# Expert tiles of a mixture-of-experts layer: four of hid's six chunks transposed by VectorE in 32x32 blocks, their low parts made by GpSimd

## The chip, the cores and the metric

The program runs on one core of a Trainium2 chip. The metric is the device time in microseconds from launch to end, the median of three runs. A profiled execution of the same program stands beside it; its span is the time from the first to the last instruction.

## The reference

A Flamingo-style block on 4 x 1024 tokens of width 256: layer norm, gated cross attention to 77 context rows, layer norm, and a feed-forward part in which each token goes to 2 of 4 experts of inner width 688, beside a shared expert. The part at issue is the routed experts:

```python
scores = softmax(xf @ gate_w.T)
topk_w, topk_idx = top_k(scores, 2)            # weights scaled to sum 1
g = silu(einsum('nh,eih->eni', xf, eg))
u = einsum('nh,eih->eni', xf, eu)
y_exp = einsum('eni,ehi->enh', g * u, ed)
y = einsum('enh,ne->nh', y_exp, comb) + shared expert
out = x + tanh(g_ffn) * y
```

## The kernel before

The first part of the program (up to about 480 us) does the attention, the shared expert and the routing table, and transposes the experts' weights into SBUF. Then `routed` works through NS = 67 tiles of 128 token slots, each with one expert. All matrix products are fp32 taken apart into a high part (rounded to fp32r) and a low part (what is left), three passes per product: high x high, high x low weights, low x high.

One tile j goes through these steps, and every engine has its own program with the steps of all tiles in order:

- GpSimd (`on_gpsimd`): `gather(j)` copies the tile's slot numbers and issues an indirect DMA that brings 128 rows into `xin[k]` (two buffers); it waits for the transposes of tile j-2 (`s_xT`).
- TensorE: `x_T(j)` transposes `xin` into PSUM (2 transposes). ScalarE: `x_hi` copies the high part; VectorE: `x_lo` subtracts the low part.
- TensorE: `gate_up(j)`, 18 matmuls into three PSUM banks. ScalarE: `sil`. VectorE: `hid` = up x sil, 128 x 688, and a second copy of the last 48 columns (`s_dup`).
- TensorE: `hidden_T(j)`, six transposes of `hid`'s chunks of 128 columns into `p_h` (four in bank 0, two in bank 1). ScalarE copies the high parts, L252 (four chunks) and L253 (two); VectorE subtracts the low parts, L298 (four chunks), L300 and L302, and then raises `s_hlo`.
- TensorE: `down(j)`, 17 matmuls of 256 columns into `p_y`. VectorE: `result(j)` (L277) scales by the slot weights into `yout[k]`. GpSimd: `add(j)` copies the slot numbers and issues an indirect DMA that adds `yout` to the output rows in HBM.

The order on TensorE in step j is `gate_up(j)`, `x_T(j+1)`, `down(j-1)`, `hidden_T(j)`. On VectorE it is `hid(j)`, `x_lo(j+1)`, `result(j-1)`, the low parts of tile j. On ScalarE it is `sil(j)`, `x_hi(j+1)`, the high parts of tile j. On GpSimd the order is `add(j)`, `gather(j+4)`, `add(j+1)`, `gather(j+5)`. Nothing reorders these; the code is written out by hand with semaphores, and tiles 2 to 65 run in a loop on each engine whose body has two tiles.

The names of the trace differ at places from those of the code, since tensors share memory: `p_gu` is shown as `p_s`, `p_x` as `p_m`, `p_h` as `p_f`, `p_y` as `p_t`.

Of the kernel before, what the change touches and what calls it, by code (L numbers as in the profile page):

```python
# [8 lines left out]
ALU = mybir.AluOpType  # L9
ACT = mybir.ActivationFunctionType  # L10
AX = mybir.AxisListType

P = 128

B, S, H = 4, 1024, 256
# [34 lines left out]
NE = N * TOPK // P  # L50
EG = 8
# [85 lines left out]
def routed(nc, v, sem, place, banks):  # L137
# [12 lines left out]
    hT = [sb(f"hT_{s}", [P, n, P], f32r) for s, n in (("hi", FC), ("lo", FC - 1))]  # L150
    p_gu, p_x, p_h, p_y = banks
    names = ("s_xT s_xhi s_xlo s_gu s_sil s_hid s_hT s_hhi s_hlo s_y s_yo s_pad "
             "s_get_at s_add_at s_add").split()
    (s_xT, s_xhi, s_xlo, s_gu, s_sil, s_hid, s_hT, s_hhi, s_hlo, s_y, s_yo, s_pad,
     s_get_at, s_add_at, s_add) = (sem("f" + n) for n in names)
# [37 lines left out]
    def on_gpsimd(pool, s_rows_out):  # L193
        gather = gathers(pool)

        def add(j, k):
            wait(pool, s_add, 16 * (j - 1))
            pool.tensor_copy(add_at[k][:, :], slot_id[:, bass.ds(j, 1)]).then_inc(s_add_at, 1)
            pool.wait_ge(s_add_at, j + 1)
            pool.wait_ge(s_yo, j + 1)  # L200

            wait(pool, s_add, 16 * j)
            settle(pool)
            pool.indirect_dma_start(out, bass.IndirectOffsetOnAxis(add_at[k][:, :], 0),  # L204
                                    yout[k][:, :], None, compute_op=ALU.add).then_inc(s_add, 16)

        gather(2, 0)
        for j in range(2):
            gather(j + 3, 1 - j)
            if j == 0:  # L210
                for s in s_rows_out:
                    pool.wait_ge(s, 16 * (NU // 2))
            add(j, j)
        with pool.Fori(1, (NS - 3) // 2) as h:
            for k in range(2):
                gather(2 * h + k + 3, 1 - k)
                add(2 * h + k, k)
        for j in range((NS - 3) // 2 * 2, NS):
            if j + 3 < NS:
                gather(j + 3, 1 - j % 2)  # L220
            add(j, j % 2)
        pool.wait_ge(s_add, 16 * NS)
# [11 lines left out]
    def on_scalar(act, down_high):  # L234
        x_hi = x_high(act)

        def step(j, k):
# [10 lines left out]
            if first:  # L248
# [3 lines left out]
            act.activation(hT[0][:, 0:4, :], p_h[0][:, :].rearrange("p (c t) -> p c t", t=P), ACT.Copy)  # L252
            act.activation(hT[0][:, 4:FC, :], p_h[1][:, 0:2 * P].rearrange("p (c t) -> p c t", t=P),  # L253
                           ACT.Copy).then_inc(s_hhi, 1)
            if first:
                down_high(2)
# [14 lines left out]
    def on_vector(dve, down_low):  # L271
# [7 lines left out]

        def step(j, k):  # L280
            last = isinstance(j, int) and j == NS - 1
            dve.wait_ge(s_sil, j + 1)
            wait(dve, s_hT, j)
            nc.vector.tensor_tensor(hid[:, 0:FF], p_gu[:, FF:2 * FF], sil[:, :], ALU.mult).then_inc(s_hid, 1)  # L284
# [10 lines left out]
            else:  # L295
                result(j - 1, 1 - k)
            dve.wait_ge(s_hhi, j + 1)
            nc.vector.tensor_tensor(hT[1][:, 0:4, :], p_h[0][:, :].rearrange("p (c t) -> p c t", t=P),  # L298
                                    hT[0][:, 0:4, :], ALU.subtract)
# [3 lines left out]
                                    hT[0][LO_AT:P, FC - 1, :], ALU.subtract).then_inc(s_hlo, 1)  # L303
            if first:
                down_low(2)
# [13 lines left out]
    def on_tensor(pe, down_weights, down_ready):  # L319
# [14 lines left out]
        def down(j, e):  # L334
            pe.wait_ge(s_hlo, j + 1)
            wait(pe, s_yo, j)
            for c in range(FC - 1):
                for q, (a, b) in enumerate(PASSES):
                    nc.tensor.matmul(p_y[:, 0:H], hT[a][:, c, :], wd[b][:, bass.ds(e * FC + c, 1), :],  # L339
                                     start=(c == 0 and q == 0), stop=False)  # L340

            for b in range(2):
                last = nc.tensor.matmul(p_y[:, 0:H], hT[0][:, FC - 1, :],  # L343
                                        wd[b][:, bass.ds(e * FC + FC - 1, 1), :], start=False, stop=(b == 1))
            last.then_inc(s_y, 1)

        def hidden_T(j):
            pe.wait_ge(s_hid, j + 1)
            wait(pe, s_hlo, j)
            for c in range(FC):  # L350
# [2064 lines left out]
```

## Time and profile before

| | us |
|---|---|
| median of 3 runs | 945.41 (942.92 to 946.67) |
| the profiled execution, its own time | 943.28 |
| its span | 941.3 |
| mean granted TensorE clock, share of full | 0.98 |
| busy in the span: TensorE / VectorE / ScalarE / GpSimd | 890.7 / 574.7 / 476.0 / 467.9 |
| busy in the 100 us from 700 to 800: TensorE / VectorE / ScalarE / GpSimd | 100.00 / 45.47 / 28.74 / 45.52 |

"PE" in the rows is TensorE's matmuls (a transpose is a matmul too), DVE is VectorE, ACT ScalarE, POOL GpSimd. A row of the timeline gives the start, the duration, the engine, the line of the kernel, the operation, the output and the input, and in brackets how long the engine had been idle before it and what ended that. Matmuls are pipelined, so their durations overlap: the chain of waits gives the time by which each one moves the chain on, which is the better measure of what they cost.

### The profile page before, as it was taken

Reading aid. Unit: us, or ns where it says so; the run is one execution under the profiler, and the core shown is the slowest. Engines: PE = TensorE matmul, PEld = TensorE weight load, DVE = VectorE, ACT = ScalarE, POOL = GpSimd, SP = SyncE. Lnnn points to the kernel's source line nnn. Section 1 sums busy time; section 2 is a strip of 40 time slices with the busy share of each in tenths; the row PEclk is TensorE's granted clock in tenths of the full one; section 3 lists DMA queues with packets and bytes.
Section 4 is the critical chain, followed back from the end, with each engine's and each line's share of the span. In section 5 each row is a group of like instructions: output and inputs, shape, how many; then the busy total and the mean of one; then the engine's idle time right before and its main releaser. Section 6 shows DMA issues by size and latency. Waiting matters only on the chain.

```text
span 941.3 us, 21873 instructions
## 1 busy us (share of the span) xinstructions
PE 890.7 (95%) x6491; PEld 797.3 (85%) x6492; DVE 574.7 (61%) x1289; ACT 476.0 (51%) x1804; POOL 467.9 (50%) x643
## 2 busy tenths in 40 slices
PE   6789999999999899998889999999999999999995
PEld 4567788888888798998779999999999999999994
DVE  5788889889888477776634444444444444444442
ACT  3999899899898234565523222222223222222221
POOL 4566667577556233667313444444444444444442
PEclk9899999999999899999989999999999999999997
DMA  5135122223212213142222222222222222222221
GB/s 178 28 120 159 61 84 88 89 74 104 64 55 92 90 36 127 65 128 87 96 71 34 39 39 39 39 45 33 45 35 43 39 39 39 39 45 33 45 37 20
DMA packets 56863, 61.72 MB, mean 66 GB/s; under 512 B 15642, under 2 KB 45183, under 8 KB 56799
## 3 DMA queue, kind: packets, MB, share of 16 engines
q1 hardware_dynamic: 42871, 43.15, 14.5%
q0 software_dynamic: 12864, 17.57, 11.3%
q8 instruction: 32, 0.52, 0.2%
q10 hardware_dynamic: 1064, 0.21, 0.1%
q14 instruction: 32, 0.26, 0.1%
HBM read 34.78 MB, written 25.82 MB: 64 GB/s over the span
## 4 chain that ended last, share of the span: by engine, by line
PE 77%; DVE 8%; ACT 6%; issue 5%; POOL 2%; DMA 1%; DVEq 0%; ACTq 0%; SPq 0%; POOLq 0%
PE p_s L329 27%; PE p_t L339 13%; PE p_f L2038 5%; PE p_f L353 5%; PE p_f L2083 4%; ACT prob L1106 3%; PE p_m L1995 3%; PE p_s L1968 2%; PE p_m L2007 2%; PE p_t L1980 2%; PE p_s L2038 2%; PE p_t L343 2%; PE p_m L1949 2%; PE p_m L314 2%; DVE xn L1450 1%
## 5 line engine op out<-in xcount | busy, mean ns | idle before, releaser
L204 POOL DMA_INDIRECT out_rows<-yout,add_at x67 | 107.1, 1598 | 196.1 <-DVE yout L277 196.1
L1106 ACT ACTIVATE prob<-p_s,negmax 128x77 f32<-128x77 f32 x512 | 161.7, 385 | 0.3
L284 DVE TENSOR_TENSOR hid<-p_s,sil 128x688 f32<-128x688 f32 x67 | 58.6, 875 | 165.7 <-ACT sil L242 105.6
L242 ACT ACTIVATE sil<-p_s 128x688 f32<-128x688 f32 x67 | 49.9, 745 | 196.1 <-PE p_s L329 196.1
L1106 ACT ACTIVATION_READ_ACCUMULATOR prob<-p_s,negmax 128x1 f32 x512 | 131.9, 269 | 0.0
L837 POOL TENSOR_TENSOR prob<-prob,rinv 128x616 f32<-128x616 f32 x64 | 78.4, 1228 | 82.9 <-DVE rinv L1494 82.9
L329 PE MATMUL p_s<-wgu_hi,fxT_hi 128*128 x402 | 111.4, 385 | 1.8 <-DVE hid L269 1.8
L329 PE MATMUL p_s<-wgu_lo,fxT_hi 128*128 x402 | 105.7, 371 | 0.0
L329 PE MATMUL p_s<-wgu_hi,fxT_lo 128*128 x402 | 105.1, 370 | 0.0
L252 ACT ACTIVATE hT_hi<-p_f 128x512 fp32r<-128x512 f32 x67 | 40.0, 597 | 124.1 <-PE p_f L353 124.1
L339 PE MATMUL p_t<-wd_hi,hT_hi 128*128 x335 | 99.5, 297 | 2.3 <-DVE hT_hi L302 2.3
L188 POOL DMA_INDIRECT xin<-xn_scratch,get_at x67 | 67.7, 1010 | 55.5 <-POOL get_at L185 51.6
L339 PE MATMUL p_t<-wd_hi,hT_lo 128*128 x335 | 94.7, 283 | 0.0
L339 PE MATMUL p_t<-wd_lo,hT_hi 128*128 x335 | 94.5, 282 | 0.0
L329 PEld LDWEIGHTS p_s<-wgu_hi,fxT_lo 128*128 128x128 f32 x402 | 72.4, 189 | 11.5
L329 PEld LDWEIGHTS p_s<-wgu_lo,fxT_hi 128*128 128x128 f32 x402 | 72.4, 189 | 11.2
L298 DVE TENSOR_TENSOR hT_lo<-p_f,hT_hi 128x512 fp32r<-128x512 f32 x67 | 46.4, 692 | 58.1 <-ACT hT_hi L253 58.1
L856 POOL TENSOR_TENSOR shT_lo<-shid,shT_hi 128x256 fp32r<-128x256 f32 x80 | 59.0, 747 | 43.9 <-ACT shT_hi L1146 43.9
L2038 PE MATMUL p_f<-xnT_hi,swgu_hi 128*128 128x256 f32 x248 | 78.2, 315 | 0.8 <-DVE shid L1509 0.8
L329 PEld LDWEIGHTS p_s<-wgu_hi,fxT_hi 128*128 128x128 f32 x402 | 69.1, 190 | 10.7 <-issue 2.0
L2038 PE MATMUL p_f<-xnT_hi,swgu_lo 128*128 128x256 f32 x248 | 70.2, 283 | 0.0
L2038 PE MATMUL p_f<-xnT_lo,swgu_hi 128*128 128x256 f32 x248 | 70.1, 283 | 0.0
(253 smaller groups left out, 2453.0 us busy)
## 6 DMA issues: line engine op xcount, KB each, us to landing
xr<-in_x SPq DMA_DIRECT2D x16, 256.0 KB, 3.1
x_scratch<-xr SPq DMA_DIRECT2D x16, 256.0 KB, 2.4
xn_scratch<-xn SPq DMA_DIRECT2D x16, 256.0 KB, 2.1
xt_scratch<-xnT SPq DMA_DIRECT2D x16, 256.0 KB, 2.1
xin<-xt_scratch SPq DMA_DIRECT2D x16, 256.0 KB, 3.3
x1in<-x_scratch SPq DMA_DIRECT2D x16, 256.0 KB, 3.1
out_rows<-syout SPq DMA_DIRECT2D x16, 256.0 KB, 2.5
raw<-in_L_ffn_ed SPq DMA_DIRECT2D x4, 688.0 KB, 4.2
```

Source lines behind the costliest of these rows:

```text
L188: pool.indirect_dma_start(xin[k][:, :], None, xn_d, bass.IndirectOffsetOnAxis(get_at[k][:, :], 0)).then_inc(s_gat[k], 16)
L204: pool.indirect_dma_start(out, bass.IndirectOffsetOnAxis(add_at[k][:, :], 0), yout[k][:, :], None, compute_op=ALU.add).then_inc(s_add, 16)
L242: act.activation(sil[:, :], p_gu[:, 0:FF], ACT.Silu).then_inc(s_sil, 1)
L284: nc.vector.tensor_tensor(hid[:, 0:FF], p_gu[:, FF:2 * FF], sil[:, :], ALU.mult).then_inc(s_hid, 1)
L298: nc.vector.tensor_tensor(hT[1][:, 0:4, :], p_h[0][:, :].rearrange("p (c t) -> p c t", t=P), hT[0][:, 0:4, :], ALU.subtract)
L329: last = nc.tensor.matmul(p_gu[:, g0:g1], fxT[a][:, c, :], wgu[b][:, bass.ds(e * KC + c, 1), g0:g1], start=(c == 0 and q == 0), stop=(c == ...
L339: nc.tensor.matmul(p_y[:, 0:H], hT[a][:, c, :], wd[b][:, bass.ds(e * FC + c, 1), :], start=(c == 0 and q == 0), stop=False)
L353: last = nc.tensor.transpose(p_h[c // 4][:, (c % 4) * P:(c % 4 + 1) * P], hid[:, c * P:(c + 1) * P], ident[:, :])
L837: pool.tensor_tensor(pr_, pr_, rinv[:, t, m * HH:(m + 1) * HH].unsqueeze(2).broadcast_to([P, HH, SK]), ALU.mult).then_inc(s_P, 1)
L856: pool.tensor_tensor(hT[1][:, c, :], hid[:, c, :], hT[0][:, c, :], ALU.subtract).then_inc(s_hlo, 1)
L1106: last = act.activation(prob[n % 2][t][:, m * PW + h * SK:m * PW + (h + 1) * SK], p_s[:, 2 * t + h // 4, col:col + SK], ACT.Exp, bias=negm ...
L2038: last = nc.tensor.matmul(bank[:, j * UT * P:(j + 1) * UT * P], swgu[w][:, k, j * SGU + c * P:j * SGU + (c + 1) * P], xns[x][:, n % 2, k, ...
```

## The change

Four of the six chunks (BY_DVE = 4) are no longer transposed by TensorE, apart from those of the last tile. VectorE does it in `squares(j)`, right behind `result(j-1)`: sixteen instructions, each of which takes 32 partitions and, in all four chunks, 32 columns, and writes them transposed into `hT32`, an SBUF tile of 128 x 512. ScalarE copies the high part from `hT32` (behind the two other chunks, and after `s_square`). GpSimd subtracts the low part in `wide_lo(j)`, which stands between `gather(j+2)` and `add(j-1)`. TensorE's `down(j)` starts with the two chunks that TensorE transposed, goes on with the high parts of the four after `s_hhi`, and ends with their four low parts after `s_wide_lo`; the number of matmuls is 17 as before. VectorE's two small subtractions, which raise `s_hlo`, stand behind the sixteen transposes. In the first tile and in the last, pieces of this order differ as the diff shows.

```diff
@@ -48,6 +48,8 @@
 
 XR = 6
 NE = N * TOPK // P
+BY_DVE = 4
+SQ = 32
 EG = 8
 NSP = NS + 1
 
@@ -204,9 +207,16 @@
             pool.indirect_dma_start(out, bass.IndirectOffsetOnAxis(add_at[k][:, :], 0),
                                     yout[k][:, :], None, compute_op=ALU.add).then_inc(s_add, 16)
 
+        def wide_lo(j):
+            pool.wait_ge(s_hhi, 2 * j + 2)
+            pool.tensor_tensor(hT[1][:, 0:BY_DVE, :], hT32[:, :, :], hT[0][:, 0:BY_DVE, :],
+                               ALU.subtract).then_inc(s_wide_lo, 1)
+
         gather(2, 0)
+        wide_lo(0)
         for j in range(2):
             gather(j + 3, 1 - j)
+            wide_lo(j + 1)
             if j == 0:
                 for s in s_rows_out:
                     pool.wait_ge(s, 16 * (NU // 2))
@@ -214,10 +224,13 @@
         with pool.Fori(1, (NS - 3) // 2) as h:
             for k in range(2):
                 gather(2 * h + k + 3, 1 - k)
+                wide_lo(2 * h + k + 1)
                 add(2 * h + k, k)
         for j in range((NS - 3) // 2 * 2, NS):
             if j + 3 < NS:
                 gather(j + 3, 1 - j % 2)
+            if j + 1 < NS - 1:
+                wide_lo(j + 1)
             add(j, j % 2)
         pool.wait_ge(s_add, 16 * NS)
 
@@ -249,9 +262,14 @@
                 down_high(1)
 
             act.wait_ge(s_hT, j + 1)
-            act.activation(hT[0][:, 0:4, :], p_h[0][:, :].rearrange("p (c t) -> p c t", t=P), ACT.Copy)
-            act.activation(hT[0][:, 4:FC, :], p_h[1][:, 0:2 * P].rearrange("p (c t) -> p c t", t=P),
+            act.activation(hT[0][:, BY_DVE:FC, :], p_h[1][:, 0:2 * P].rearrange("p (c t) -> p c t", t=P),
                            ACT.Copy).then_inc(s_hhi, 1)
+            if last:
+                act.activation(hT[0][:, 0:BY_DVE, :], p_h[0][:, :].rearrange("p (c t) -> p c t", t=P),
+                               ACT.Copy).then_inc(s_hhi, 1)
+            else:
+                act.wait_ge(s_square, j + 1)
+                act.activation(hT[0][:, 0:BY_DVE, :], hT32[:, :, :], ACT.Copy).then_inc(s_hhi, 1)
             if first:
                 down_high(2)
 
@@ -277,10 +295,20 @@
             nc.vector.tensor_scalar(yout[k][:, :], p_y[:, 0:H], slots[:, bass.ds(j, 1)], None,
                                     ALU.mult).then_inc(s_yo, 1)
 
+        def squares(j):
+            dve.wait_ge(s_hid, j + 1)
+            wait(dve, s_wide_lo, j)
+            src = hid[:, 0:BY_DVE * P].rearrange("p (c i) -> p c i", i=P)
+            for a in range(0, P, SQ):
+                for b in range(0, P, SQ):
+                    done = nc.vector.transpose(out=hT32[b:b + SQ, :, a:a + SQ], in_=src[a:a + SQ, :, b:b + SQ])
+            done.then_inc(s_square, 1)
+
         def step(j, k):
             last = isinstance(j, int) and j == NS - 1
             dve.wait_ge(s_sil, j + 1)
             wait(dve, s_hT, j)
+            wait(dve, s_square, j)
             nc.vector.tensor_tensor(hid[:, 0:FF], p_gu[:, FF:2 * FF], sil[:, :], ALU.mult).then_inc(s_hid, 1)
 
             nc.vector.tensor_tensor(hid[:, (FC - 1) * P + LO_AT:(FC - 1) * P + LO_AT + FT],
@@ -294,13 +322,17 @@
                 down_low(1)
             else:
                 result(j - 1, 1 - k)
-            dve.wait_ge(s_hhi, j + 1)
-            nc.vector.tensor_tensor(hT[1][:, 0:4, :], p_h[0][:, :].rearrange("p (c t) -> p c t", t=P),
-                                    hT[0][:, 0:4, :], ALU.subtract)
+            if not last:
+                squares(j)
+            dve.wait_ge(s_hhi, 2 * j + 1)
             nc.vector.tensor_tensor(hT[1][:, 4, :], p_h[1][:, 0:P], hT[0][:, 4, :], ALU.subtract)
 
             nc.vector.tensor_tensor(hT[0][LO_AT:P, FC - 1, :], p_h[1][LO_AT:P, P:2 * P],
                                     hT[0][LO_AT:P, FC - 1, :], ALU.subtract).then_inc(s_hlo, 1)
+            if last:
+                dve.wait_ge(s_hhi, 2 * j + 2)
+                nc.vector.tensor_tensor(hT[1][:, 0:BY_DVE, :], p_h[0][:, :].rearrange("p (c t) -> p c t", t=P),
+                                        hT[0][:, 0:BY_DVE, :], ALU.subtract).then_inc(s_wide_lo, 1)
             if first:
                 down_low(2)
         tiles(dve, step)
@@ -334,20 +366,27 @@
         def down(j, e):
             pe.wait_ge(s_hlo, j + 1)
             wait(pe, s_yo, j)
-            for c in range(FC - 1):
-                for q, (a, b) in enumerate(PASSES):
-                    nc.tensor.matmul(p_y[:, 0:H], hT[a][:, c, :], wd[b][:, bass.ds(e * FC + c, 1), :],
-                                     start=(c == 0 and q == 0), stop=False)
-
+            for q, (a, b) in enumerate(PASSES):
+                nc.tensor.matmul(p_y[:, 0:H], hT[a][:, FC - 2, :], wd[b][:, bass.ds(e * FC + FC - 2, 1), :],
+                                 start=(q == 0), stop=False)
             for b in range(2):
-                last = nc.tensor.matmul(p_y[:, 0:H], hT[0][:, FC - 1, :],
-                                        wd[b][:, bass.ds(e * FC + FC - 1, 1), :], start=False, stop=(b == 1))
+                nc.tensor.matmul(p_y[:, 0:H], hT[0][:, FC - 1, :], wd[b][:, bass.ds(e * FC + FC - 1, 1), :],
+                                 start=False, stop=False)
+            pe.wait_ge(s_hhi, 2 * j + 2)
+            for c in range(BY_DVE):
+                for b in range(2):
+                    nc.tensor.matmul(p_y[:, 0:H], hT[0][:, c, :], wd[b][:, bass.ds(e * FC + c, 1), :],
+                                     start=False, stop=False)
+            pe.wait_ge(s_wide_lo, j + 1)
+            for c in range(BY_DVE):
+                last = nc.tensor.matmul(p_y[:, 0:H], hT[1][:, c, :], wd[0][:, bass.ds(e * FC + c, 1), :],
+                                        start=False, stop=(c == BY_DVE - 1))
             last.then_inc(s_y, 1)
 
         def hidden_T(j):
             pe.wait_ge(s_hid, j + 1)
             wait(pe, s_hlo, j)
-            for c in range(FC):
+            for c in range(0 if isinstance(j, int) and j == NS - 1 else BY_DVE, FC):
                 if c == FC - 1:
                     pe.wait_ge(s_dup, j + 1)
                 last = nc.tensor.transpose(p_h[c // 4][:, (c % 4) * P:(c % 4 + 1) * P], hid[:, c * P:(c + 1) * P],
```

The program of VectorE around one tile of the loop, before (names as in the trace; `yout_177` and `yout_178` are the two `yout` buffers):

```order
L284 TENSOR_TENSOR hid<-p_s,sil 128x688 [waits fs_hT,fs_sil]
L286 TENSOR_TENSOR hid<-p_s,sil 128x48
L262 REGISTER_ALU
L263 TENSOR_TENSOR fxT_lo<-p_m,fxT_hi 128x256 [waits fs_xhi]
L174 ISA [waits fs_y]
L277 ISA [waits fs_add]
L277 TENSOR_SCALAR yout_178<-p_t,slots 128x256
L298 TENSOR_TENSOR hT_lo<-p_f,hT_hi 128x512 [waits fs_hhi]
L300 TENSOR_TENSOR hT_lo<-p_f,hT_hi 128x128
L302 TENSOR_TENSOR hT_hi<-p_f,hT_hi 64x128
```

And the same place with the change (`hT_189` is `hT32`):

```order
L312 TENSOR_TENSOR hid<-p_s,sil 128x688 [waits fs_square,fs_hT,fs_sil]
L314 TENSOR_TENSOR hid<-p_s,sil 128x48
L280 REGISTER_ALU
L281 TENSOR_TENSOR fxT_lo<-p_m,fxT_hi 128x256 [waits fs_xhi]
L177 REGISTER_ALU [waits fs_y]
L295 ISA [waits fs_add]
L295 TENSOR_SCALAR yout_177<-p_t,slots 128x256
L304 STREAM_TRANSPOSE hT_189<-hid 32x4x32 [waits fs_wide_lo,fs_hid]
L304 STREAM_TRANSPOSE hT_189<-hid 32x4x32 x15
L327 ISA
L328 TENSOR_TENSOR hT_lo<-p_f,hT_hi 128x128 [waits fs_hhi]
L330 TENSOR_TENSOR hT_hi<-p_f,hT_hi 64x128
L167 REGISTER_ALU
```

The large subtraction of 512 columns is gone and the sixteen transposes stand in its place, ahead of the two small subtractions that they had stood behind.

GpSimd's program for one tile of the loop, before (`xin`, `get_at`: the gather; `yout`, `add_at`: the add):

```order
L185 ISA [waits fs_xT]
L185 COPY get_at_182<-slot_id 128x1
L186 REGISTER_ALU
L188 DMA xin_175<-xn_scratch,get_at_182 128x256 [waits fs_get_at]
L198 ISA [waits fs_add]
L198 COPY add_at_185<-slot_id 128x1
L174 REGISTER_ALU [waits fs_yo,fs_add_at]
L204 DMA out_rows<-yout_178,add_at_185 4224x256 [waits fs_add]
```

And with the change:

```order
L188 ISA [waits fs_xT]
L188 COPY get_at_182<-slot_id 128x1
L189 REGISTER_ALU
L191 DMA xin_175<-xn_scratch,get_at_182 128x256 [waits fs_get_at]
L211 ISA
L212 TENSOR_TENSOR hT_lo<-hT_189,hT_hi 128x512 [waits fs_hhi]
L201 ISA [waits fs_add]
L201 COPY add_at_185<-slot_id 128x1
L177 REGISTER_ALU [waits fs_yo,fs_add_at]
L207 DMA out_rows<-yout_178,add_at_185 4224x256 [waits fs_add]
```

A subtraction that waits for `s_hhi` now stands behind the gather and ahead of the copy and the DMA of the add, and so ahead of the next gather too.

## Rows read from the trace of the kernel before

**Rows 1.** The chain of waits in one tile: start us, us, what

```profile
606.75 0.22 PE p_m L314 x2
606.97 1.77 PE p_t L339 x15
608.74 0.24 PE p_t L343 x2
608.98 0.66 PE p_f L353 x6
609.64 3.73 PE p_s L329 x18
```

**Rows 2.** Timeline of one tile, VectorE and TensorE

```profile
700.15 0.88 DVE L284 TENSOR_TENSOR hid<-p_s,sil 128x688 f32<-128x688 f32 x1 [2.40 <-ACT sil L242]
...
700.94 0.20 DVE L286 TENSOR_TENSOR hid<-p_s,sil 128x48 f32<-128x48 f32 x1
...
701.40 0.82 PE L353 MATMUL p_f<-ident,hid 128*128 128x128 f32 x6
701.82 0.48 DVE L277 TENSOR_SCALAR yout<-p_t,slots 128x256 f32<-128x256 f32 x1 [0.35 <-PE p_t L343]
...
703.77 0.28 DVE L300 TENSOR_TENSOR hT_lo<-p_f,hT_hi 128x128 fp32r<-128x128 f32 x1
...
704.07 0.29 DVE L302 TENSOR_TENSOR hT_hi<-p_f,hT_hi 64x128 fp32r<-64x128 f32 x1
```

**Rows 3.** Timeline of one tile, GpSimd

```profile
703.29 1.60 POOL L204 DMA_INDIRECT out_rows<-yout,add_at  x1 [2.84 <-DVE yout L277]
704.33 0.76 POOL L185 COPY get_at<-slot_id 128x1 int32 x1
705.88 1.01 POOL L188 DMA_INDIRECT xin<-xn_scratch,get_at  x1 [0.80 <-POOL get_at L185]
706.89 0.20 POOL L198 COPY add_at<-slot_id 128x1 int32 x1
```

**Rows 4.** DMA issues: name, queue, count, us from issue to landing

```profile
xin<-xn_scratch,get_at POOLq DMA_INDIRECT x67, 2.8
```

**Rows 5.** VectorE's groups by shape: count, busy us, mean ns, idle before

```profile
L298 DVE TENSOR_TENSOR hT_lo<-p_f,hT_hi 128x512 fp32r<-128x512 f32 x67 | 46.4, 692 | 58.1 <-ACT hT_hi L253 58.1
...
L300 DVE TENSOR_TENSOR hT_lo<-p_f,hT_hi 128x128 fp32r<-128x128 f32 x67 | 18.8, 281 | 0.0
...
L1754 DVE SCALAR_TENSOR_TENSOR pick<-seen,eq 128x128 f32<-128x128 f32 x2 | 0.9, 469 | 0.1
```

**Rows 6.** ScalarE's groups by shape

```profile
L1131 ACT ACTIVATE xnT_hi<-xin 128x512 fp32r<-128x512 f32 x16 | 10.5, 654 | 0.0
```

**Rows 7.** GpSimd's groups by shape

```profile
L850 POOL TENSOR_TENSOR xnT_lo<-xin,xnT_hi 128x512 fp32r<-128x512 f32 x16 | 20.6, 1288 | 2.5 <-ACT xnT_hi L1131 2.5
```

**Rows 8.** TensorE's timeline, three idle stretches and what came behind them

```profile
444.06 1.11 PE L2343 MATMUL p_m<-at_val,at_row 128*128 128x204 f32 x8 [1.62 <-POOL at_val L1035]
...
472.23 0.65 PE L2144 MATMUL p_s<-ident,raw 128*128 128x128 f32 x4 [2.01 <-DMA raw<-in_L_ffn_eu]
...
481.76 0.89 PE L329 MATMUL p_s<-wgu_hi,fxT_hi 128*128 x3 [1.79 <-DVE hid L269]
```

**Rows 9.** Windows of 2 us: busy us of PE, PEld, DVE, ACT, POOL; PEclk; DMA

```profile
444.00:446.00 2.00, 1.94 (x17) 1.97 (x18) 0.34 (x1) 0.26 (x1) 2.00 (x3) 1.00 0.56 181
472.00:474.00 2.00, 1.77 (x11) 1.80 (x12) 0.45 (x1) 0.60 (x1) 0.00 (x0) 0.68 0.83 321
482.00:484.00 2.00, 2.00 (x8) 1.73 (x8) 0.00 (x0) 0.00 (x0) 0.00 (x0) 0.74 0.24 82
```

**Rows 10.** The chain of waits near its end, at the lower clock

```profile
929.01 0.14 issue
929.15 2.82 PE p_t L339 x15
931.97 0.44 PE p_t L343 x2
```

More of the change, by code:

```diff
@@ L150, in routed @@
     hT = [sb(f"hT_{s}", [P, n, P], f32r) for s, n in (("hi", FC), ("lo", FC - 1))]
+    hT32 = sb("hT32", [P, BY_DVE, P])
     p_gu, p_x, p_h, p_y = banks
     names = ("s_xT s_xhi s_xlo s_gu s_sil s_hid s_hT s_hhi s_hlo s_y s_yo s_pad "
-             "s_get_at s_add_at s_add").split()
+             "s_get_at s_add_at s_add s_square s_wide_lo").split()
     (s_xT, s_xhi, s_xlo, s_gu, s_sil, s_hid, s_hT, s_hhi, s_hlo, s_y, s_yo, s_pad,
-     s_get_at, s_add_at, s_add) = (sem("f" + n) for n in names)
+     s_get_at, s_add_at, s_add, s_square, s_wide_lo) = (sem("f" + n) for n in names)
     s_gat = [sem(f"fs_gat{k}") for k in range(2)]
```

## The prediction

> **What bounds the kernel now.** I read the chain of waits first. Through the routed tiles it never leaves TensorE: two transposes of rows 0.22, fifteen and two matmuls of the down product 1.77 + 0.24, six transposes of hid 0.66, eighteen matmuls of gate and up 3.73, with no gap [rows 1]. One tile is 6.61 us, and 67 of them are nearly half of the span. The other engines wait for TensorE in each tile, so time on them is free as long as they keep up. The question is therefore not what TensorE saves but how long the new path from hid to the down product is.
>
> **What is removed.** TensorE loses four of six transposes, 4 x 0.66 / 6 = 0.44 per tile [rows 1]. If everything else hid, a tile would be 6.17. VectorE loses its subtraction of 512 columns, 0.69 [rows 5].
>
> **What a transpose instruction costs.** The trace has none. Sixteen stand in a row per tile, each over 128 elements of a partition. The nearest row is VectorE's 128x128 subtraction, 0.281 [rows 5]. Per element it streams (692 - 281) / 384 = 1.07 ns [rows 5], so 128 elements alone are 0.14: the lower bound, if all the fixed part overlapped. The upper bound is the dearest instruction on 128x128, 0.469 [rows 5], 0.49 with its gap. Whether neighbours overlap matters as much. L286 starts at 700.94, 0.09 before L284 ends (700.15 + 0.88), so neighbours that write the same partitions overlap [rows 2]. L302, which writes from partition 64 on, starts at 704.07, 0.02 after L300 ends (703.77 + 0.28) and without any semaphore to wait for [rows 2]. Each of the sixteen writes another block of 32 partitions than the one in front. I take them as L302: 0.28 + 0.02 = 0.30 from start to start, 4.80 for sixteen. If they overlapped, it would be 0.28 - 0.08 = 0.20, 3.20 for sixteen.
>
> The Trainium skill speaks against this change at this very place. Its page VectorE: DVE Perf Modes, section Two Vector instructions with no wait between them, says that an instruction whose output starts in another group of 32 partitions than the last output to that memory is held until every earlier one has finished. By that rule all sixteen are held; the trace agrees in the one gap of 0.02 [rows 2]. The same page, section The three transpose paths, gives 311 ns for a VectorE transpose of 128x128 bf16; no run here shows it. As an estimate from that page sixteen would be 16 x 0.33 = 5.3, and the forecast below some 30 us longer.
>
> **The new chains, from one tile's transposes to the next tile's.** Three loops now run through squares, since `result(j-1)` stands ahead of `squares(j)` on VectorE and needs the whole `down(j-1)`.
>
> 1. By `s_hlo`. Transposes 4.80; the two small subtractions queued behind them 0.59 (703.77 to 704.36 [rows 2]); VectorE to TensorE 0.14 [rows 10]; all of down 2.01 [rows 1]; from down's end to L277 0.42 (701.40 to 701.82 [rows 2]); L277 0.48 [rows 2]. Sum 8.44.
> 2. By the low parts. 4.80; ScalarE's copy of 512 columns from SBUF 0.65 [rows 6]; GpSimd's subtraction of 512 columns 1.29 [rows 7]; the last four matmuls 4/17 x 2.01 = 0.47; 0.42 and 0.48; handovers, of which the last is 0.14 and the two others I estimate at 0.05 each. Sum 8.35.
> 3. By the gather. On GpSimd `wide_lo(j)` is a new wait, and behind it stand the copy and DMA of `add(j-1)` and the copy and DMA of `gather(j+3)`, on which `x_T(j+3)` waits. From its end: copy 0.20, wait before a DMA 0.79 (705.09 to 705.88), add to next copy 1.04 (703.29 to 704.33), copy 0.76, wait 0.79 [rows 3], issue to landing 2.8 [rows 4]: 6.38. Before, the add followed L277 directly and the gather landed well ahead of its use: issued at 705.88 [rows 3], landed at 708.7 [rows 4], for an x_T that comes two tiles behind the one that started at 701.40 - 2.01 - 0.22 = 699.17, so at 712.4. Now x_T, down, 0.42, L277, transposes, ScalarE, GpSimd and handovers follow: 0.22 + 2.01 + 0.42 + 0.48 + 4.80 + 0.65 + 1.29 + 0.15 = 10.02. This loop closes two tiles on (`x_T(j+3)` is issued ahead of `down(j+1)`, whose result frees `squares(j+2)`), so the period is 16.40 / 2 = 8.20.
>
> The three are nearly alike, the first is longest: 8.44. It exceeds TensorE's 6.17 by 2.27, which TensorE idles. VectorE's own work, 4.80 + 0.59 + 0.88 + 0.20 + 0.48 = 6.95 and x_lo, which on half the columns of L298 takes under its 0.69, lies inside. The number of matmuls in down is the same, its order too costs nothing. ScalarE's wide copy costs 0.05 more than before and lies on loop 2 alone.
>
> **The clock.** TensorE is now granted full speed throughout this stage. Rows show what idling does: behind an idle stretch of 2.01 and one of 1.79 [rows 8] the windows have a granted clock of 0.68 and 0.74 of full [rows 9], that is a fall to the lower level (1.2 for 2.4 GHz) within them; behind one of 1.62 the window shows 1.00 [rows 8, 9]. The new 2.27 of each tile lies mostly in one piece, between gate_up's end and x_T or down. At the lower clock down takes 2.82 + 0.44 = 3.26 [rows 10] against 2.01, so a tile that is hit costs 1.25 on loops 1 and 3. A fall also stretches gate_up, which shortens the next idle stretch, so I take every second tile: 0.63 per tile, with 0 and 1.25 as bounds.
> The Trainium skill, TensorE: Matmul & The Clock Gate, section The two states you'll see, has the same two levels, the lower behind idleness; the rows above agree.
>
> **The sum.** Per tile 8.44 + 0.63 = 9.07, which is 2.46 more than 6.61. Tiles 0 to 65 have squares, so 65 periods: +160. The profiled execution was 943.3, so 1103. The median, 945.4, is 2 above it, so I predict 1105. The last tile stays on TensorE's transposes, and its down may start earlier by the order of the low parts; under 1 us, left out.
>
> **Rivals.**
> - Clock stays up: 8.44, +1.83 x 65 = +119, 1064. For it: 1.62 left the clock alone, and x_T cuts the idle stretch in two. Against it: 1.79 and 2.01 did not. 12%.
> - Transposes overlap (0.20 each): loop 1 is 6.84, loop 2 6.75, but loop 3 is (3.20 + 11.60) / 2 = 7.40; +0.79 x 65 = +51, 997. The idle stretches are then half as long. For it: L286. Against it: L302. 15%.
> - The clock falls in every tile, in gate_up too, or a transpose costs well over 0.30. With TensorE always at the lower level a tile would be 2 x 6.17 = 12.3; halfway between this and 8.44 is 10.4, +3.78 x 65 = +246, 1191. At 0.49 per transpose loop 1 would be 11.5, even further. 18%.
> - Faster than before. The one way is that sixteen transposes cost little enough for loop 3, the last to stay long, to be under 6.61: 16.40 - 4.80 = 11.60 is its fixed part, so sixteen must be under 1.62, 0.10 each. That needs twice the streaming rate of the trace's rows and no fixed part at all: 0.07 each makes 1.10, loop 3 is 6.35, -0.26 x 65 = -17, 928. No row supports it. 3%.
>
> **How the numbers follow.** The forecast (held transposes at about 0.30, clock falling in some tiles) has 51%, its own range 1075 to 1150. A change of 0.5% is about what a measurement of this kernel can tell from none. With 1% for no change by luck of the loops, 3% for faster, slower has 96%. For 8 in 10 the range takes in the rival with the clock up, most of the overlapping one, and the lower side of the dear one: 1000 to 1185.
>
> **What the profile after will show.** The sixteen transposes' mean duration and their distance from start to start (0.30; at 0.20 the second rival holds). TensorE's matmul groups with idle time before x_T (from the gather) and before down (from VectorE's small subtraction), 2 to 3 us per tile in sum. The granted clock of the routed stage under 1.00, at about 0.85. GpSimd's gather issued only about 4 us after its subtraction's end. The period between two L277, 9.07. I am wrong if L277's period is under 7.5, if TensorE is still busy without gaps, or if its idle time hangs on something that none of the three loops names.

## The result

The changed kernel takes 1182.38 us (median of 4, 1179.39 to 1184.58), against 945.79 for the kernel before on the same chips: a ratio of 1.2506, 95% interval [1.2467, 1.2545]. That is 237 us slower. The prediction was 1105 us with a range of 1000 to 1185, so the result lies 2.6 us inside the upper end. Its profiled execution spans 1179.8 us, against 941.3, with a mean granted clock of 0.889 against 0.980.

The distance from one `result` (L277, now L295) to the next, averaged over forty tiles in the middle of the loop, went from 6.61 to 10.24 us. 65 x 3.63 is 236 us, so the whole difference lies in the loop over tiles.

### The profile page after: what moved, and what is told of

It is laid out like the page before. It is cut to its first block, busy times and chain, and to the rows that moved or that the text cites. A ratio compares the mean times of both kernels' runs of the same rounds, so it can differ in the third digit from the quotient of the medians.

```text
span 1179.8 us, 22625 instructions
## 1 busy us (share of the span) xinstructions
PE 984.2 (83%) x6227; PEld 859.7 (73%) x6228; DVE 848.4 (72%) x2279; ACT 478.0 (41%) x1804; POOL 546.9 (46%) x709
## 4 chain that ended last, share of the span: by engine, by line
issue 44%; PE 24%; POOL 16%; DVE 7%; ACT 6%; POOLq 2%; DMA 1%; DVEq 0%; ACTq 0%
POOL xin L191 5%; POOL out_rows L207 5%; PE p_f L2077 4%; ACT prob L1145 3%; PE p_f L2122 3%; POOL get_at L188 3%; PE p_m L2034 2%; PE p_m L2046 2%; PE p_t L2019 2%; PE p_s L2007 2%; PE p_s L2077 2%; PE p_m L1988 1%; DVE xn L1489 1%; DVE th L1543 1%; PE p_s L2122 1%
## 5 line engine op out<-in xcount | busy, mean ns | idle before, releaser
L304 DVE STREAM_TRANSPOSE hT<-hid 32x128 f32<-32x128 f32 x1056 | 319.1, 302 | 13.5
L212 POOL TENSOR_TENSOR hT_lo<-hT,hT_hi 128x512 fp32r<-128x512 f32 x66 | 84.2, 1275 | 300.4 <-ACT hT_hi L272 300.4
L272 ACT ACTIVATE hT_hi<-hT 128x512 fp32r<-128x512 f32 x66 | 41.5, 629 | 335.2 <-DVE hT L304 335.2
L370 PE MATMUL p_t<-wd_hi,hT_hi 128*128 x67 | 37.6, 561 | 142.3 <-DVE hT_hi L330 138.9
L295 DVE TENSOR_SCALAR yout<-p_t,slots 128x256 f32<-128x256 f32 x67 | 32.4, 484 | 144.0 <-PE p_t L382 144.0
L370 PEld LDWEIGHTS p_t<-wd_hi,hT_hi 128*128 128x128 f32 x67 | 18.7, 278 | 157.9 <-issue 157.9
L265 ACT ACTIVATE hT_hi<-p_f 128x256 fp32r<-128x256 f32 x67 | 25.7, 384 | 215.5 <-PE p_f L392 215.5
L378 PE MATMUL p_t<-wd_hi,hT_hi 128*128 x268 | 109.9, 411 | 0.0
L378 PE MATMUL p_t<-wd_lo,hT_hi 128*128 x268 | 109.9, 411 | 0.0
L378 PEld LDWEIGHTS p_t<-wd_lo,hT_hi 128*128 128x128 f32 x268 | 87.3, 326 | 0.0
L378 PEld LDWEIGHTS p_t<-wd_hi,hT_hi 128*128 128x128 f32 x268 | 87.3, 326 | 0.0
```

The source lines that it names most:

```text
L212: pool.tensor_tensor(hT[1][:, 0:BY_DVE, :], hT32[:, :, :], hT[0][:, 0:BY_DVE, :], ALU.subtract).then_inc(s_wide_lo, 1)
L304: done = nc.vector.transpose(out=hT32[b:b + SQ, :, a:a + SQ], in_=src[a:a + SQ, :, b:b + SQ])
L370: nc.tensor.matmul(p_y[:, 0:H], hT[a][:, FC - 2, :], wd[b][:, bass.ds(e * FC + FC - 2, 1), :], start=(q == 0), stop=False)
L378: nc.tensor.matmul(p_y[:, 0:H], hT[0][:, c, :], wd[b][:, bass.ds(e * FC + c, 1), :], start=False, stop=False)
```

## The profile after

The groups of the new instructions from the page (line, engine, operation, count, busy us, mean ns, idle before and what ended it):

```profile
L304 DVE STREAM_TRANSPOSE hT<-hid 32x128 f32<-32x128 f32 x1056 | 319.1, 302 | 13.5
L212 POOL TENSOR_TENSOR hT_lo<-hT,hT_hi 128x512 fp32r<-128x512 f32 x66 | 84.2, 1275 | 300.4 <-ACT hT_hi L272 300.4
L272 ACT ACTIVATE hT_hi<-hT 128x512 fp32r<-128x512 f32 x66 | 41.5, 629 | 335.2 <-DVE hT L304 335.2
```

A transpose is 0.302 us. There are sixteen per tile.

Busy time by engine in 100 us of the routed stage (PE, PEld, DVE, ACT, POOL, then the granted clock and the DMA share):

```profile
700.00:800.00 100.00, 80.34 (x390) 70.36 (x390) 69.34 (x214) 18.37 (x39) 41.91 (x50) 0.83 0.16 26
```

TensorE was busy for all of such a window before. Now it idles a fifth of it, although part of its work runs at the lower clock: 0.83 is the mean of a stretch where it had been 1.00. Within a tile the granted clock is at one of two levels (down at 0.50, then gate_up and the idle stretch at 1.00, then down at 0.50 again):

```profile
700.50:703.00 2.50, 2.50 (x14) 2.50 (x13) 1.29 (x3) 0.21 (x1) 1.58 (x3) 0.50 0.00 0
704.00:707.50 3.50, 3.50 (x18) 2.84 (x16) 3.37 (x12) 0.30 (x1) 1.01 (x2) 1.00 0.45 75
708.50:710.00 1.50, 0.00 (x0) 0.00 (x0) 1.40 (x5) 0.63 (x2) 0.00 (x0) 1.00 0.00 0
711.00:713.00 2.00, 2.00 (x12) 2.00 (x11) 0.98 (x3) 0.00 (x0) 1.08 (x3) 0.50 0.00 0
```

What one tile looks like on the timeline, from one `result` to the next:

```profile
703.90 0.48 DVE L295 TENSOR_SCALAR yout<-p_t,slots 128x256 f32<-128x256 f32 x1 [2.11 <-PE p_t L382]
...
704.30 5.04 DVE L304 STREAM_TRANSPOSE hT<-hid 32x128 f32<-32x128 f32 x16
...
709.37 0.29 DVE L328 TENSOR_TENSOR hT_lo<-p_f,hT_hi 128x128 fp32r<-128x128 f32 x1
709.37 0.63 ACT L272 ACTIVATE hT_hi<-hT 128x512 fp32r<-128x512 f32 x1 [5.07 <-DVE hT L304]
709.67 0.29 DVE L330 TENSOR_TENSOR hT_hi<-p_f,hT_hi 64x128 fp32r<-64x128 f32 x1
...
710.09 1.27 POOL L212 TENSOR_TENSOR hT_lo<-hT,hT_hi 128x512 fp32r<-128x512 f32 x1 [4.28 <-ACT hT_hi L272]
...
710.23 0.57 PE L370 MATMUL p_t<-wd_hi,hT_hi 128*128 x1 [2.19 <-DVE hT_hi L330]
...
713.16 0.78 PE L382 MATMUL p_t<-wd_hi,hT_lo 128*128 x4
...
713.77 0.38 PE L392 MATMUL p_f<-ident,hid 128*128 128x128 f32 x2
...
714.19 0.48 DVE L295 TENSOR_SCALAR yout<-p_t,slots 128x256 f32<-128x256 f32 x1 [2.20 <-PE p_t L382]
```

This is the first loop of the prediction, step by step. L295 to the first transpose 0.40; sixteen transposes to L328 5.07 (704.30 to 709.37); the two small subtractions 0.59, to 709.96; to the first matmul of down 0.27; down until the next transpose of TensorE, 3.54 (710.23 to 713.77); to L295 0.42. The sum is 10.29, all of the distance between these two L295. Down took 1.77 + 0.24 = 2.01 before [rows 1]. Its matmuls stand 0.21 apart here and stood 0.12 apart there: they run at the lower clock. It is so nearly everywhere: down's matmuls of the four chunks take 411 ns in the mean of the whole program (L378 on the page), and took 282 to 297 before (L339). The down product of [rows 10], from which the prediction took its 3.26 us, ran at the lower clock only in its later part. Its first eight matmuls start 0.12 apart (0.21 behind the very first), as at full clock, and the others 0.19 to 0.22 (granted clock 1.00 from 929.5 to 930, and 0.50 from 930.5 on):

```profile
929.84 0.29 PE L339 MATMUL p_t<-wd_hi,hT_lo 128*128 x1
929.96 0.30 PE L339 MATMUL p_t<-wd_hi,hT_hi 128*128 x1
930.08 0.39 PE L339 MATMUL p_t<-wd_lo,hT_hi 128*128 x1
930.27 0.41 PE L339 MATMUL p_t<-wd_hi,hT_lo 128*128 x1
930.49 0.41 PE L339 MATMUL p_t<-wd_hi,hT_hi 128*128 x1
```

So 3.26 is no price of a whole down at the lower clock; that price is the 3.54 of this timeline.

Who waited for whom between 560 and 1140 us (total, times, longest):

```profile
ACT hT_hi L272 <- DVE hT L304: 289.3, 57, 5.1
...
DVE yout L295 <- PE p_t L382: 122.8, 57, 2.2
PE p_t L370 <- DVE hT_hi L330: 119.9, 56, 2.3
...
PEld p_m L346 <- DMA xin<-xn_scratch,get_at: 20.3, 57, 1.6
```

TensorE waits for VectorE's small subtraction in 56 of 56 tiles, 2.1 us each, and VectorE for down, 2.2 us each. The gather's DMA, the third loop, is a short wait beside them, 0.36 us in the mean for the weight load of x_T: in a tile this long it has landed when gate_up ends or shortly after, so x_T follows with hardly a gap and TensorE's idle time lies in one piece behind it (2.19 ahead of L370 at 710.23).

## The experiments

Each changes the changed kernel, at the lines shown. "Period" is the mean distance of `result` to `result` over forty tiles in the middle of the loop, read from the profiled execution. The runs with fewer transposes, with four large ones and with sixteen that stay in their partitions leave out part of the work, so `hT32` does not hold the whole transposed chunks; they tell what a shorter or cheaper `squares` would be worth, and are no kernels to use.

**Filler on TensorE.** Does the clock cost anything, or is the chain simply 10.2 long?

```diff
+            if not fixed:
+                for i in range(9):
+                    nc.tensor.matmul(p_h[0][:, 0:512], wgu[0][:, 0, 0:P], wgu[0][:, 1, 0:512], start=True, stop=True)
             if not (fixed and j == 0):
                 down(j - 1, expert(1 - k))
```

> The changed kernel with nine idle-time matmuls of 512 columns (about 1.9 us, into a bank that nobody reads) on TensorE ahead of down(j-1) in each tile of the loop, where it now idles 2.2 us. Theory (the clock): TensorE's idling makes the clock fall in every tile, and this alone takes the tile from 5.07 + 0.62 + 0.27 + 2.01 + 0.42 + 0.40 = 8.79 us to 10.24; with the filler the clock stays at 1.00 and the period is 8.8, 1180 - 65 x 1.45 = 1086 us. Rival (the chain alone is 10.2 long, whatever the clock): 1175 to 1185 us, or more by the filler.

Measured: 1131.06 us, ratio 1.198 [1.193, 1.203], period 9.39. The clock did stay up:

```profile
700.00:800.00 100.00, 92.40 (x514) 77.89 (x513) 76.77 (x237) 20.78 (x43) 44.66 (x53) 1.00 0.17 29
```

but the period missed 8.8. TensorE's timeline shows why: x_T waits for the gather (idle 0.51 after gate_up), and the nine fillers, 2.17 us, stand between it and down.

```profile
701.55 0.79 PE L361 MATMUL p_s<-wgu_hi,fxT_lo 128*128 x3
702.85 0.44 PE L346 MATMUL p_m<-ident,xin 128*128 128x128 f32 x2 [0.51 <-DMA xin<-xn_scratch,get_at]
703.04 2.33 PE L419 MATMUL p_f<-wgu_hi 128*128 128x512 f32 x9
705.21 0.28 PE L370 MATMUL p_t<-wd_hi,hT_hi 128*128 x1
```

So they were put on the loop by the gather, (5.07 + 11.60 + 2.17) / 2 = 9.42, which then binds. The same kernel with eight fillers, ahead of `x_T(j + 1)` instead:

> As the run with nine filler matmuls, but eight of them (8 x 0.241 = 1.93 us) and ahead of x_T, where TensorE would only wait for the gather, so that they do not stand between the gather's landing and down. Theory: the nine kept the clock at 1.00 and cost 2.17 us on the loop by the gather, (5.07 + 11.60 + 2.17) / 2 = 9.42, measured 9.39. Ahead of x_T they cost nothing there; the loop by s_hlo binds, 5.07 + 0.62 + 0.14 to 0.27 + 2.01 + 0.42 + 0.40 = 8.7 to 8.8, clock at or near 1.00, 946 + 65 x 2.15 = 1085 us. Rival (fillers always cost what they last): about 1130 us as before.

Measured: 1097.43 us, ratio 1.162 [1.158, 1.165], period 8.86, clock 1.00:

```profile
700.00:800.00 100.00, 97.25 (x532) 82.44 (x531) 80.94 (x251) 21.12 (x44) 46.97 (x56) 1.00 0.18 31
```

The period is near the 8.7 to 8.8 of the chain. The time is 12 us above the forecast of 1085, of which 65 x 0.10 = 6.5 are the period (8.86 against 2.15 + 6.61 = 8.76); the rest lies outside the loop's middle. Extra work on TensorE made the kernel 85 us faster. This is the direct price of the clock, 10.24 - 8.86 = 1.38 us per tile. It all lies in down: from its first matmul to the next transpose it takes 3.55 us in the changed kernel and 2.17 here (means of 35 tiles), and no other step of the loop differs by more than 0.01.

**How much filler is needed.** The same with `range(3)`:

> The changed kernel with three filler matmuls (3 x 0.24 = 0.72 us) ahead of x_T in place of eight. Eight kept the clock at 1.00 and the period at 8.86 where TensorE idles 2.6 us per tile without them. Theory (the fall has an edge, as the run with fourteen transposes shows, whose idle time of 2.1 us per tile did not bring it about): three are enough, 8.7 to 8.9 per tile, 1080 to 1100 us. Rival (the clock's cost shrinks in proportion to the idle time): between 8.9 and 10.2, 1110 to 1160 us.

Measured: 1095.96 us, ratio 1.162 [1.158, 1.165], period 8.86. Three do what eight did:

```profile
700.00:800.00 100.00, 85.82 (x476) 70.38 (x477) 80.37 (x248) 22.67 (x47) 47.77 (x57) 1.00 0.17 29
```

**Two transposes fewer.** Is the clock's cost a fixed amount on top of the chain?

```diff
+            blocks = [(a, b) for b in range(0, P, SQ) for a in range(0, P, SQ)]
+            for a, b in blocks if isinstance(j, int) else blocks[:14]:
```

> The changed kernel with fourteen of the sixteen transposes in each tile of the loop (two of the block moves are left out, so an eighth of the chunks holds old data). This takes 0.63 us out of every loop that runs through squares. Theory A (the clock's share of a tile is a fixed 1.5 us on top of the chain): the period goes from 10.24 to 9.61, 1182 - 41 = 1141 us. Theory B (the clock falls in every tile because the idle stretch and the low stretch feed each other; a little less idle time frees some of the tiles from the fall altogether): more than 0.63 goes, the granted clock rises above 0.84, the period is 8.4 to 9.0, 1060 to 1100 us.

Measured: 1059.93 us, ratio 1.122 [1.119, 1.125], period 8.24, clock 1.00 through the middle of the loop:

```profile
700.00:800.00 100.00, 84.41 (x478) 69.74 (x477) 78.96 (x242) 24.05 (x51) 51.77 (x61) 1.00 0.19 31
```

Theory B held, and the gain is even larger than it forecast: the period lies below its 8.4 to 9.0. An eighth of the transposes takes 2.00 us from the period: 0.63 are its own, 1.37 the clock's, which is all of it at once. 8.86 - 0.63 = 8.23 is what the filler runs give for the chain.

**Eight transposes, and GpSimd's order.** Is the loop by the gather real? First `blocks[:8]`, then the same with this on GpSimd:

```diff
                 gather(2 * h + k + 3, 1 - k)
-                wide_lo(2 * h + k + 1)
                 add(2 * h + k, k)
+                wide_lo(2 * h + k + 1)
```

> The changed kernel with eight of the sixteen transposes in each tile of the loop (the other half is left out, so half of the four chunks holds old data). Theory (three loops): loop by s_hlo is 8 x 0.315 = 2.52 + 0.62 + 0.27 + 2.01 + 0.42 + 0.40 = 6.24, but the loop by the gather is (2.52 + 11.6) / 2 = 7.06, so the period is 7.1, TensorE waits for the gather's DMA ahead of x_T, and the time is 943 + 65 x 0.45 = 972 us. Rival (the gather is never a bound): the period is TensorE's 6.2 to 6.4, 915 to 930 us.

> As the run with eight transposes (half left out), and GpSimd does add(j-1) ahead of wide_lo(j) instead of behind it. Theory (three loops): the loop by the gather is gone, what is left is 6.2 to 6.5 per tile, 920 to 935 us. Rival (the gather is no bound in the run with eight transposes either): no difference between the two.

Measured: 986.94 us, ratio 1.046 [1.041, 1.050], period 7.15 for the first; 944.16 us, ratio 1.000 [0.998, 1.002], period 6.50 for the second. In the first x_T waits for the gather (weights and matmuls of L346, 560 to 860 us):

```profile
PEld p_m L346 <- DMA xin<-xn_scratch,get_at: 23.0, 26, 1.2
...
PE p_m L346 <- DMA xin<-xn_scratch,get_at: 13.9, 21, 0.8
```

In the second TensorE is nearly always busy:

```profile
700.00:800.00 100.00, 98.11 (x603) 87.81 (x603) 72.93 (x217) 31.16 (x62) 64.65 (x77) 1.00 0.24 39
```

GpSimd's order alone is worth 0.65 per tile where the gather binds. Both times are above the forecasts, 972 and 920 to 935. In the first, some 6 us of the miss are the period (7.15 against 7.06) and the rest lies outside the loop's middle (the first `result` distance is 8.95). The second's period of 6.50, the upper end of its forecast, is that of its profiled execution, which took 937.76 us and was the fastest of nine; the other eight took 942.76 to 946.09, and what they spent more is not known.

These two runs and the one with fourteen go through the blocks in another order (`for b` outside and `for a` inside), which matters for the sixteen that stay, below: four in a row write the same 32 partitions, and each reads from another group than the one in front. They start 0.315 apart all the same, eight in 2.53 to L328:

```profile
703.61 2.50 DVE L304 STREAM_TRANSPOSE hT<-hid 32x128 f32<-32x128 f32 x8
706.14 0.29 DVE L328 TENSOR_TENSOR hT_lo<-p_f,hT_hi 128x128 fp32r<-128x128 f32 x1
```

**Four transposes of 128 partitions.** What if the transposes cost next to nothing?

```diff
-            for a in range(0, P, SQ):
-                for b in range(0, P, SQ):
-                    done = nc.vector.transpose(out=hT32[b:b + SQ, :, a:a + SQ], in_=src[a:a + SQ, :, b:b + SQ])
+            for c in range(BY_DVE):
+                done = nc.vector.transpose(out=hT32[:, c, :], in_=src[:, c, :])
```

> The changed kernel with four transposes of 128x128 per tile in place of sixteen of 32x128: each turns its 32x32 blocks where they stand and moves none to another group of partitions, so that part of the transpose is left out. The same number of elements per partition and instruction is 4 x 128 instead of 16 x 128. Theory: about 0.29 each, 1.16 for four (0.9 if these overlap, since they write the same partitions), loop by the gather (1.16 + 11.6) / 2 = 6.38, TensorE 6.17, so about 6.4: 930 us, faster than before. Rival (the cost lies in the waits that were added and not in the transposes' duration): above 950 us.

Measured: 936.44 us, ratio 0.991 [0.989, 0.993], period 6.47, close to the 6.4 and 930 us of the theory. The instruction is no dearer than one of 32 partitions, and four take 0.88 in all:

```profile
L303 DVE STREAM_TRANSPOSE hT<-hid x264: 268/270/304, 494.5 to 917.8; 128x128 f32<-128x128 f32 x132
```

So all of the loss hangs on the transposes' duration; what the change moved beside them costs little. But even transposes as cheap as this bring 0.14 of the 0.44 that TensorE saves. The chain of waits of this run shows where the rest stays:

```profile
702.15 3.83 PE p_s L360 x18
705.97 0.22 PE p_m L345 x2
...
708.21 0.22 PE p_f L391 x2
708.42 0.10 issue
708.53 4.05 PE p_s L360 x18
```

gate_up is 3.83 in one tile and 0.10 + 4.05 in the next, against 3.73 [rows 1]. The loop's body has two tiles, and this alternates with it: that the instructions of the branch and the registers stand there and were hidden behind six transposes is likely, but it was not tried. A gap of about 0.25 marked "issue" ahead of gate_up in every second tile is also in the runs with fourteen, with eight and with three fillers.

**Sixteen that stay in their partitions.** Why is one transpose 0.315 from start to start?

```diff
-                    done = nc.vector.transpose(out=hT32[b:b + SQ, :, a:a + SQ], in_=src[a:a + SQ, :, b:b + SQ])
+                    done = nc.vector.transpose(out=hT32[a:a + SQ, :, b:b + SQ], in_=src[a:a + SQ, :, b:b + SQ])
```

> The changed kernel with its sixteen transposes of 32x128 as they are in number, size and input, but each writes its blocks to the 32 partitions that it read (the move to another group of partitions is left out), so that four in a row read and write the same partitions. Theory (an instruction that starts in another group of partitions than the one in front is held until that one has finished): twelve of sixteen overlap and start 0.20 apart, four are held, about 0.30 apart: 12 x 0.2 + 4 x 0.3 = 3.6 in place of 5.07; the loop by the gather is then (3.6 + 11.7) / 2 = 7.65, 7.6 to 7.8 per tile, 1005 to 1020 us. Rival (a 32-partition transpose costs 0.31 from start to start wherever it writes): 1182 us, no change.

Measured: 1019.68 us, ratio 1.081 [1.078, 1.084], period 7.69. A transpose is 0.260 in the median, and sixteen take 3.57 with 3.60 to the next instruction:

```profile
L304 DVE STREAM_TRANSPOSE hT<-hid x1056: 256/260/309, 491.5 to 997.7; 32x128 f32<-32x128 f32 x176
```

```profile
699.77 3.57 DVE L304 STREAM_TRANSPOSE hT<-hid 32x128 f32<-32x128 f32 x16
703.37 0.29 DVE L328 TENSOR_TENSOR hT_lo<-p_f,hT_hi 128x128 fp32r<-128x128 f32 x1
```

That is the 3.6 of the rule, and 7.69 the 7.65 of the loop by the gather. Where four in a row keep to their partitions they start 0.20 apart in the mean, and where the group changes 0.27. The changes of group cost the other 1.5 us per tile. It is the change from one instruction to the next that counts, in what is written or in what is read, and not that data move between groups. In the changed kernel the group written changes each time; in the runs with eight and fourteen the one written stays for four in a row and the one read changes; both are 0.315 apart. Four of the sixteen in the changed kernel (those with a = b) write the partitions that they read, and start no earlier behind their neighbour than the others. In these runs neighbours overlap only where neither changes.

**The small subtractions first.** VectorE's L328 and L330, which raise `s_hlo`, ahead of `squares(j)`:

> The changed kernel with VectorE's two small subtractions, and so s_hlo, ahead of the sixteen transposes. The loop by s_hlo is then 5.07 + 0.05 + 0.63 (ScalarE's wide copy) + 0.14 + twelve wide matmuls, and the loop by GpSimd's subtraction is the longest: 5.07 + 0.62 less, that is 5.04 + 0.05 + 0.63 + 0.05 + 1.28 + 0.14 + 0.47 + 0.42 + 0.40 = 8.5 at full clock. Theory B (as of the run with fourteen transposes): down's five first matmuls run early and break TensorE's idle stretch, loops are 0.3 shorter, clock falls in part of the tiles: period 8.5 to 9.3, 1065 to 1120 us. Rival (the order on VectorE does not matter, as all three loops are nearly alike and the clock keeps its fall in every tile): 1175 to 1185 us.

This did not settle. Two timed runs of the same kernel gave 1181.97 and 1144.19 us, with mean granted clocks of 0.890 and 0.942, so no ratio is given, and how far the clock falls differs from run to run here. Both are above the 1065 to 1120 of theory B and only the longer one lies in the rival's 1175 to 1185, so the two executions decide nothing. The profiled one is the longer, with a period of 10.24; there the clock falls in every tile, though TensorE starts down early and its idle time comes in two pieces, 0.7 us ahead of x_T and 1.4 us within down. Of the shorter one there is no trace, so what this order is worth stays open.

**Transposes ahead of the result.** `squares(j)` before `result(j - 1)` on VectorE opens the loop through down; first with the add ahead of `wide_lo` on GpSimd, too:

```diff
+            if not last:
+                squares(j)
             if first:
                 down_low(1)
             else:
                 result(j - 1, 1 - k)
-            if not last:
-                squares(j)
```

> The changed kernel with squares(j) ahead of result(j-1) on VectorE, and add(j-1) ahead of wide_lo(j) on GpSimd. The loop squares - down - result - squares is then no longer closed through result. Theory: VectorE's own work is what is left, 0.79 + 0.11 + 0.41 + 5.07 + 0.40 + 0.62 and some handovers, 7.4 to 7.6 per tile, with the clock falling in part of the tiles or not at all: 995 to 1030 us. It is the floor of sixteen transposes of 0.3 us, and above the 945 of before. Rival (a new loop: result(j-1) behind squares(j) holds back down(j) by s_yo and add): 1060 us or more.

Measured: 1139.09 us, ratio 1.206 [1.202, 1.209], period 9.56 at a clock of 0.98. The theory failed; it looked at VectorE's order and not at who waits for the result behind it. This is the rival's case, a new loop, though by another way than the rival named. The timeline has the new loop:

```profile
702.05 5.05 DVE L304 STREAM_TRANSPOSE hT<-hid 32x128 f32<-32x128 f32 x16 [1.86 <-POOL hT_lo L212]
...
707.13 0.48 DVE L295 TENSOR_SCALAR yout<-p_t,slots 128x256 f32<-128x256 f32 x1
...
708.60 1.60 POOL L207 DMA_INDIRECT out_rows<-yout,add_at  x1 [4.53 <-DVE yout L295]
...
709.66 1.85 POOL L212 TENSOR_TENSOR hT_lo<-hT,hT_hi 128x512 fp32r<-128x512 f32 x1
...
711.61 5.05 DVE L304 STREAM_TRANSPOSE hT<-hid 32x128 f32<-32x128 f32 x16 [1.86 <-POOL hT_lo L212]
```

Transposes 5.08, L295 0.48, to the add's DMA 0.99, to L212 1.06, L212 1.85, and to the next transposes, which need `hT32` free, 0.10: 9.56. `wide_lo` stood behind an add that waited for a result that stood behind the transposes. With GpSimd's order as in the changed kernel:

> As the run with squares(j) ahead of result(j-1) on VectorE, but with GpSimd's order as in the changed kernel (wide_lo(j) ahead of add(j-1)). In that run a new loop of 9.56 went squares - result - add's DMA on GpSimd - wide_lo - squares (which waits for hT32 to be free). Theory: with wide_lo ahead of the add this loop is squares 5.07 + ScalarE 0.68 + GpSimd 1.33 + 0.1 = 7.2, and VectorE's own work binds: 0.79 + 0.11 + 0.41 + 5.07 + 0.40 + 0.62 = 7.4, with handovers 7.4 to 7.8, 995 to 1025 us at full clock. Rival (the clock falls again, or another wait of VectorE for TensorE closes a loop): 8.5 or more per tile, over 1060 us.

Measured: 1018.51 us, ratio 1.080 [1.077, 1.083], period 7.61, clock 1.00, as the theory had it. VectorE never stops for anything but 0.31 us of `sil`:

```profile
700.38 5.04 DVE L304 STREAM_TRANSPOSE hT<-hid 32x128 f32<-32x128 f32 x16
705.46 0.48 DVE L295 TENSOR_SCALAR yout<-p_t,slots 128x256 f32<-128x256 f32 x1
705.86 0.28 DVE L328 TENSOR_TENSOR hT_lo<-p_f,hT_hi 128x128 fp32r<-128x128 f32 x1
706.15 0.29 DVE L330 TENSOR_TENSOR hT_hi<-p_f,hT_hi 64x128 fp32r<-64x128 f32 x1
706.75 0.88 DVE L312 TENSOR_TENSOR hid<-p_s,sil 128x688 f32<-128x688 f32 x1 [0.31 <-ACT sil L255]
```

This is the best full version found, 164 us faster than the changed kernel and still 75 slower than before. It is bound by VectorE, of whose 7.61 the transposes are 5.08.

## Why the prediction was right, and where it was off

- *The number:* 1105 against 1182, a change of 160 forecast and of 237 measured. The stated range held by 2.6 us, and the forecast's own range, 1075 to 1150, did not. Inside at all is partly luck: the upper end was set to take in the lower side of a rival, and that rival came true.
- *What bounds it now, and that slack is free:* right. The time followed the new chain, not TensorE's savings.
- *A transpose is 0.30 from start to start, held by the change of partitions:* right to 6%. It is 0.302 and a gap of 0.013, 5.07 for sixteen against 4.80. The reason is shown by the sixteen that stay (3.60), and the runs with the other order of blocks add that a change of the group read holds as well. The overlapping rival, 0.20, is what the sixteen that stay do.
- *The loop by `s_hlo`, 8.44:* it is the one that binds, and measures 8.86 without the clock. Transposes +0.27, handover 0.22 in the mean and not 0.14, and down at full clock 2.17 and not 2.01, of which about 0.1 is its first matmul behind a wait; against that, L295 counts for 0.40 and not 0.48, since the first transpose starts before it ends. This is 27 us of the 77 by which 1105 missed.
- *The loop by the gather, (transposes + 11.60) / 2:* right where it can be seen. 7.06 against 7.15 with eight, 7.65 against 7.69 with the sixteen that stay, 9.42 against 9.39 with fillers on it, and it went away with GpSimd's order.
- *The clock, "so I take every second tile: 0.63 per tile":* this is the step that failed. It falls in every tile, and takes 1.38, or 90 us of the 237 (the filler run has 85); the other 50 of the missing 77 are here. The mechanism was named and its two bounds, 0 and 1.25, were given; the value was set between them by an argument (a fall stretches gate_up and so shortens the next idle stretch) that the runs refute for this kernel. Gate_up is not stretched, since it runs at full clock; and with 14 transposes or three fillers the cost is 0, with 16 it is whole. What the argument overlooked is in the trace: the fall lengthens the tile, the gather lands in time, x_T no longer cuts the idle stretch in two, and so 2.2 us of idling in one piece come back in each tile. With fourteen x_T waits for the gather, 1.0 us in the mean of the tiles between 560 and 860 us, and down for 0.1 to 1.0 in one tile of four; with three fillers, the waits that are left are 0.4 and 0.8. That this feedback is what makes the edge fits these rows; no run changed the gather alone at sixteen, so it is not shown. The upper bound, 1.25, was too low too: [rows 10] were read as a down at the lower clock throughout, and nearly half of its matmuls ran at full clock. All of down at the lower clock is 3.54, and the price against 2.17 is 1.38.
- *The rival "in every tile":* it was given 18% and 1191 us, and 1182 is its case, but not as it was told: the clock falls in every tile, yet gate_up runs at full clock, as the windows above show. Its price was made as halfway to 12.3, which comes out near by luck; the right one was 8.86 + 3.55 - 2.17 (down at the lower clock in place of down at full clock behind a wait) = 10.24.
- *The faster rival:* its threshold was loop 3 under 6.61. The run with four transposes is that case, at 0.88 us, and is 0.9% faster (without the moves between partitions that the real transpose needs).
- *What the profile would show:* idle time of 2 to 3 us per tile (2.2), a clock at about 0.85 (0.83) and the gather about 4 us after the subtraction's end (3.6) came so. That part of the idle time would stand before x_T did not: it is all before down.

## What to carry to other kernels

Moving work off the bound engine pays only if every loop through the new path stays shorter than the old period; here the longest was 8.86 us against 6.61 before any fall of the clock. Put the whole loop together, including whatever is queued behind the new waits, on all engines. When TensorE starts to idle regularly, price the lower clock both in every period and in none, since these kernels, nearly alike, went to one or the other; the cheapest test of its share is filler work in the idle stretch, on no loop that binds.

## What was not expected of the hardware

- The clock's cost has an edge: two transposes fewer, or 0.72 us of filler, and it went from 1.38 us per tile to none. It is not a matter of idle time in sum: in the run with the transposes ahead of the result and the add first, TensorE was busy for 226.6 of the 300 us from 560 to 860, that is idle for 2.3 us per tile, in pieces of about 1.3 and 1.0, at a clock of 0.98. The changed kernel idles 2.2 per tile in one piece, at 0.84 in the same stretch. What decides between them is not shown; the run with the small subtractions first, with pieces of 1.4 and 0.7, came out at 0.84 in the one execution that was profiled.
- Neighbouring VectorE transposes of 32x128 start 0.20 us apart as long as each reads and writes the groups of 32 partitions of the one before, and 0.315 apart if either changes every time. The size in partitions costs next to nothing: one of 128x128 takes 0.270 in the median, one of 32x128 that stays 0.260. The first of four that stay takes 0.30, like all sixteen of the changed kernel.
- GpSimd's L212, 1.28 us otherwise, is shown with 1.85 right behind the issue of an indirect DMA; spans on that engine are rough, but the next transposes did wait that long.
